# Routed expert works of two sizes, 256 and 128 rows, and three sets of split weights behind one staging tile

## The reference, cut to what matters

```python
scores = jnp.sqrt(jax.nn.softplus(flat @ gate_w))
_, indices = jax.lax.top_k(scores + gate_bias, 2)
weights = jnp.take_along_axis(scores, indices, axis=1)
weights = weights / jnp.clip(weights.sum(axis=-1, keepdims=True), 1e-06)
...
def _expert(xf, W1, W2, W3):                  # 192 -> 768 -> 192
    gate = jnp.minimum(xf @ W1, LIMIT)
    up = jnp.clip(xf @ W3, -LIMIT, LIMIT)
    return jax.nn.silu(gate) * up @ W2
y = _expert(flat, w1s, w2s, w3s)              # shared expert, all tokens
# plus, for each token, its two of eight experts, weighted
```

## Time and profile before

| | us |
|---|---|
| median of 3 runs | 557.76 |
| lowest, highest | 555.09, 557.76 |
| the profiled execution | 561.62 |
| its span | 559.8 |
| PE, DVE, ACT, POOL busy in it | 505.7, 375.3, 256.3, 229.4 |
| first routed matmul to the last result home | 130.6 to 317.95 |

### The profile page before, as it was taken

The page is one execution under the profiler, slowest core; times in us unless marked ns, Lnnn a source line. Parts: engine busy times, 40 slices in busy tenths (PEclk is TensorE's granted clock), DMA queues, the critical chain, the costliest instruction groups (busy, mean ns, idle before and its releaser), DMA issues.

```text
span 559.8 us, 9739 instructions
## 1 busy us (share of the span) xinstructions
PE 505.7 (90%) x3430; PEld 480.4 (86%) x3430; DVE 375.3 (67%) x892; ACT 256.3 (46%) x531; POOL 229.4 (41%) x194
## 2 busy tenths in 40 slices
PE   5799868779999999999999979999797788999996
PEld 5789768679999999999999869877576778999995
DVE  1576777356666666665666496799996766666665
ACT  0357471205554455544554214895761255353431
POOL 1404104715566657765666502488662100041300
PEclk9999998879999999999999989999998799999999
DMA  8750002753466567656673424000010200000001
GB/s 346 255 229 2 1 1 78 301 167 89 162 240 235 204 231 251 252 198 199 239 274 104 129 70 156 2 1 1 16 64 1 78 0 1 2 0 1 2 1 64
DMA packets 22634, 65.03 MB, mean 116 GB/s; under 512 B 6432, under 2 KB 15008, under 8 KB 19776
## 3 DMA queue, kind: packets, MB, share of 16 engines
q1 hardware_dynamic: 20192, 59.55, 30.4%
q0 software_dynamic: 2400, 4.93, 2.5%
HBM read 55.50 MB, written 8.97 MB: 115 GB/s over the span
## 4 chain that ended last, share of the span: by engine, by line
PE 72%; DVE 14%; issue 4%; ACT 4%; DMA 3%; POOL 2%; SPq 0%; DVEq 0%; POOLq 0%; ACTq 0%
PE psum L666 23%; PE psum L686 12%; PE psum L449 10%; PE psum L1077 4%; PE psum L466 3%; PE psum L833 3%; PE psum L1092 2%; PE psum L854 2%; PE psum L1109 2%; DVE AT L2029 2%; PE psum L1134 2%; DVE Y L1613 2%; PE psum L915 2%; PE psum L473 2%; DVE OW L2012 1%
## 5 line engine op out<-in xcount | busy, mean ns | idle before, releaser
L729 POOL TENSOR_TENSOR w0l<-stage,w0h 128x768 fp32r<-128x768 f32 x34 | 62.5, 1838 | 87.9 <-ACT w0h L713 82.0
L686 PE MATMUL psum<-w0d,a0h 128*128 128x192 f32 x492 | 86.8, 332 | 8.9 <-issue 6.6
L686 PEld LDWEIGHTS psum<-w0d,a0h 128*128 128x128 f32 x492 | 81.3, 194 | 11.4 <-issue 8.7
L761 DVE TENSOR_SCALAR a0t<-psum 128x256 f32<-128x256 f32 (+1 forms) x114 | 50.7, 445 | 47.8 <-PE psum L666 40.3
L740 ACT ACTIVATE psum<-psum 128x256 f32<-128x256 f32 x96 | 35.3, 368 | 85.0 <-PE psum L666 76.7
L666 PE MATMUL psum<-XWh,w0h 128*128 128x256 f32 x192 | 56.3, 293 | 0.0
L666 PE MATMUL psum<-XWh,w0t 128*128 128x256 f32 x192 | 54.4, 283 | 0.0
L666 PE MATMUL psum<-XWl,w0h 128*128 128x256 f32 x192 | 53.9, 281 | 0.0
L666 PE MATMUL psum<-XWl,w0t 128*128 128x256 f32 x192 | 53.8, 280 | 0.0
L666 PE MATMUL psum<-XWh,w0l 128*128 128x256 f32 x192 | 53.8, 280 | 0.0
L449 PE MATMUL psum<-X,w1h 128*128 128x384 f32 x144 | 49.6, 344 | 1.8 <-DVE a1hf L604 1.8
(11 more groups left out here) (261 smaller groups left out, 1264.6 us busy)
## 6 DMA issues: line engine op xcount, KB each, us to landing
stage<-moe0w SPq DMA_DIRECT2D x18, 1536.0 KB
w0d<-moe0d SPq DMA_DIRECT2D x18, 576.0 KB, 4.0
stage<-moe1w SPq DMA_DIRECT2D x4, 1056.0 KB, 5.0
marked_rows<-zero SPq DMA_DIRECT2D x4, 772.0 KB, 13.2
patch<-patches SPq DMA_DIRECT2D x4, 768.0 KB, 7.8
XR<-marked_rows SPq DMA_DIRECT2D x16, 192.0 KB, 3.6
G<-slots_out SPq DMA_DIRECT2D x6, 288.0 KB, 4.6
XR<-marked_rows SPq DMA_DIRECT2D x16, 65.0 KB, 3.8
```

Source lines behind the costliest of these rows:

```text
L686: last = nc.tensor.matmul(dst, A0["h"][qpar][:, fc, t * P:(t + 1) * P], W0[par]["down"][:, fc, :], start=(fc == these[0]), stop=(fc == the ...
L729: ins = engine.tensor_tensor(W0[par]["l"][:, mat, :], src, W0[par]["h"][:, mat, :].bitcast(F32), ALU.subtract)
L761: nc.vector.tensor_scalar(A0["t"][fc % 2][:, 0:width], bank[2 + fc % 2][:, 0:width], LIMIT, -LIMIT, ALU.min, ALU.max).then_inc(S0["clip_re ...
```

## The change

**Two sizes.** `WT` is 128 now, and the experts get whole blocks of 128 rows, `PARTS` = 25 of them. Eight works take two blocks each (wide, even numbers), nine take one (lone, odd numbers); they alternate, 17 in all. 3200 rows are computed where 4096 were. A longer table on VectorE (`wide_parts`, `lone_parts`, `experts`, `places`) finds the expert and the first block (`part`) of each work; SyncE reads both from it.

**A lone work** has its operands the other way round: the 128 rows are stationary and 384 columns of weights move (`e_rows_gate_up`), 20 matmuls. The product then lies with rows on partitions and is turned by six transposes (`e_turn`, in two halves) that ScalarE copies to `hT` (`e_turned`), before the down matmuls.

**Weights.** There are three sets of split weights (`w00`, `w01`, `w02`) and one staging tile of four pieces of 384 KB, each with a load and a semaphore of its own. Piece i of work n is loaded when the low part of piece i of work n - 1 is made. The low parts are counted by engine (`w_lo_pool`, `w_lo_dve`) and shared out by `low_engines`. Weights are loaded and split one work further ahead. The loops are written out, and the DMAs of the lone works' results are one each.

```diff
-WT = 256
-WORKS = (PICKS * TOK - E0) // WT + E0
-SLOTS = WORKS * WT
+WT = P
+PARTS = (PICKS * TOK - E0) // WT + E0
+WIDE = E0
+LONE = PARTS - 2 * WIDE
+WORKS = WIDE + LONE
+SLOTS = (PARTS + 2) * WT
...
+        def low_engines(n):
+            return {0: "pppp", 1: "vvvv", 2: "vvpp"}.get(n, "pppv" if n % 2 else "ppvv")
...
             def load_weights(n):
-                if n >= 2:
-                    sp.wait_ge(S["w_lo"], 4 * (n - 1))
...
+                for i in range(4):
+                    sp.wait_ge(*((S["w_lo_pool"], lows("p", n - 1, i)) if low_engines(n - 1)[i] == "p" else
+                                 (S["w_lo_dve"], lows("v", n - 1, i))))
+                    w = moe0w[0] if n == TAIL else moe0w[bass.ds(experts[n], 1)].rearrange("e p c -> (e p) c")
+                    sp.dma_start(stage[:, i, :], w[:, i * F0:(i + 1) * F0]).then_inc(ld_stage[i], 16)
...
             load_rows(1)
             load_rows(2)
-            for n in range(2, WORKS + 1):
-                if n > 2:
-                    load_rows(n)
-                load_weights(n + 1)
-                load_down(n)
-            load_down(TAIL)
+            load_weights(3)
+            load_rows(3)
+            for n in range(1, WORKS + 1):
+                if n + 3 <= TAIL:
+                    load_weights(n + 3)
+                if n + 3 <= WORKS:
+                    load_rows(n + 3)
+                load_down(n + 1)
...
+        def e_rows_gate_up(pe, u, n):
+            pe.wait_ge(x_lo, n)
+            for half in range(2):
...
+                for mat in range(2):
+                    wait_lows(pe, n, 2 * mat + 1)
+                    for i, (x, w) in enumerate(e_operands(1, None, W0[n % SETS],
+                                                          (slice(0, P), mat, slice(half * LH, (half + 1) * LH)))):
+                        last = nc.tensor.matmul(bank[2 * mat + half][:, 0:LH], x, w, start=(i == 0), stop=(i == 4))
+                last.then_inc(S0["gu_ready"], 1)
...
+            for n in range(1, WORKS + 1):              # ScalarE
+                u = units(n)
+                if n % 2:
+                    if n > 1:
+                        e_split_next(act, n + 2, 0)
+                        e_split_next(act, n + 2, 1)
+                    e_rows_silu(act, u, 0)
...
+            for n in range(3, TAIL + 1):               # GpSimd
                 if n > 4:
-                    pool.wait_ge(st_y[n % 2], 16 * (n - 4 + n % 2))
-                e_split_low(nc.gpsimd, pool, n, n % 2, range(3))
-                pool.wait_ge(S0["w_lo"], 4 * n + 3)
+                    pool.wait_ge(st_y[n % 2], sent(n - 4))
+                e_split_low(nc.gpsimd, pool, n)
+                pool.wait_ge(S0["w_lo_pool"], lows("p", n, 3))
                 if n > 3:
                     send_home(n - 3)
...
-            experts()
             e_product(dve, 0, 0, 5, CHW)
-            e_dve(dve, FC0, 1, CHW, None, None, None)
-            e_split_low(nc.vector, dve, 1, 1)
+            e_dve(dve, FC0, 1, CHW, None, {1: wide_parts, 2: lone_parts, 3: experts})
+            e_split_low(nc.vector, dve, 1)
+            places()
...
+            for n in range(1, WORKS + 1):              # VectorE
...
+                if n < WORKS:
+                    e_rows_low(dve, n + 1)
+                if n + 2 <= TAIL:
+                    e_split_low(nc.vector, dve, n + 2)
+                if n > 1:
+                    e_copy(dve, n - 1)
```

More of the change, by code:

```diff
@@ L53 @@
 XW1 = D + 1
-ZROWS = SLOTS // P // 4
+ZERO = 3
+ZROWS = SLOTS // P // ZERO
 SPARE = P * ZROWS
+RING3 = 3
 RING = (5, 6, 2)
@@ L208, in tower @@
         base = sb("base", [P, E0])
+        twos = sb("twos", [P, E0])
+        rest = sb("rest", [P, E0])
+        ends = sb("ends", [P, 2, 2, E0])
+        shift2 = sb("shift2", [P, 2, E0])
+        order = sb("order", [P, 2, LONE])
+        place = sb("place", [P, 2, LONE])
+        held = sb("held", [P, 2, LONE])
+        part = sb("part", [P, 2, LONE], I32)
         slot = sb("slot", [P, TILES * E0])
@@ L667, in e_gate_up, with e_turn, e_down @@
                 last.then_inc(S0["gu_ready"], 1)
[L669 to L673 removed]
+        def e_rows_gate_up(pe, u, n):
+            pe.wait_ge(x_lo, n)
+            for half in range(2):
+                if n == 1:
+                    pe.wait_ge(S0["silu_ready"], u + (half - 1))
+                else:
+                    pe.wait_ge(S0["h_ready"], u + (half - 2))
+                pe.wait_ge(S0["clip_ready"], u + (half - 1))
+                for mat in range(2):
[4 more added lines that the diff above has]
+                last.then_inc(S0["gu_ready"], 1)
+        def e_turn(pe, u, n, half):
+            pe.wait_ge(S0["h_ready"], u + (half + 1))
+            if half:
+                pe.wait_ge(h_out, turned_in(n) - 1)
+            for k in range(3):
+                last = nc.tensor.transpose(bank[7][:, k * P:(k + 1) * P], hR[:, half * LH + k * P:half * LH + (k + 1) * P],
+                                           ident)
+            last.then_inc(h_T, 1)
+        def e_down(pe, u, qpar, n, par, shared, ready, these=range(MOE0.fc)):
+            lone = not shared and n % 2
+            if lone:
+                pe.wait_ge(h_out, turned_in(n))
+            else:
+                pe.wait_ge(S0["h_ready"], u + these[-1] + 1)
+            pe.wait_ge(ld_w2[par], ready)
+            for t in range(3 if shared else 2 - par):
                 if shared:
@@ L715, in e_split_act, with e_split_next, e_split_low @@
                                  ACT.Copy).then_inc(S0["w_hi"], 1)
-        def e_split_low(engine, eng, n, par, parts=range(4)):
-            for i in parts:
+        def e_split_next(act, n, i):
+            if n <= TAIL:
+                e_split_act(act, n, i)
+        def e_split_low(engine, eng, n):
+            me = "p" if engine is nc.gpsimd else "v"
+            done = S0["w_lo_pool" if me == "p" else "w_lo_dve"]
+            w = W0[n % SETS]
+            for i in range(4):
+                if low_engines(n)[i] != me:
+                    continue
@@ L731, in e_split_low @@
-                ins.then_inc(S0["w_lo"], 1)
-        def e_act(act, u, width, following, rows, between={}, these=range(MOE0.fc)):
-            routed = width == WT
+                    dst = w["t"][64:P, mat, :]
+                    engine.tensor_tensor(dst, src[64:P], dst.bitcast(F32), ALU.subtract).then_inc(done, 1)
+                else:
+                    engine.tensor_tensor(w["l"][:, mat, :], src, w["h"][:, mat, :].bitcast(F32),
+                                         ALU.subtract).then_inc(done, 1)
@@ L736, in e_act @@
+        def e_act(act, u, width, between={}, these=range(MOE0.fc)):
+            routed = width == 2 * WT
             for fc in these:
                 act.wait_ge(S0["gu_ready"], u + (fc + 1))
-                if not routed and not (isinstance(u, int) and u == 0 and fc < 2):
+                if not routed and not (u == 0 and fc < 2):
                     act.wait_ge(S0["h_ready"], u + (fc - 1))
@@ L1014, in _ @@
+            e_gate_up(pe, TAIL_U, TAIL, 0, 2, range(AHEAD, AHEAD + 1))
+            e_down(pe, units(WORKS), 1, WORKS, 1, False, loaded(WORKS))
+            e_gate_up(pe, TAIL_U, TAIL, 0, 2, range(AHEAD + 1, FC0))
+            e_down(pe, TAIL_U, 0, TAIL, 0, True, loaded(TAIL), range(AHEAD, FC0))
             transposes(2, 0)
@@ L1318, in project @@
+            e_act(act, TAIL_U, CHW, these=range(AHEAD, FC0))
             def project(g):
@@ new lines, in _, with reached @@
+            lone_to, wide_to, lone_from, wide_from = (ends[:, i, k, :] for i in range(2) for k in range(2))
+            grid = [P, 2, LONE, E0]
+            def reached(to, side):
+                return nc.vector.tensor_tensor(
+                    to.rearrange("p (k w e) -> p k w e", k=2, e=E0),
+                    counts[:, 0:LONE].unsqueeze(1).unsqueeze(3).to_broadcast(grid),
+                    ends[:, side].unsqueeze(2).to_broadcast(grid), ALU.is_ge)
+            above, within = (rk[i][:, 0:2 * LONE * E0] for i in range(2))
```

456 lines of the change are left out of this document (267 added, 189 removed).

## The result

| | before | after |
|---|---|---|
| median, us | 557.6 | 579.28 |
| lowest, highest | 555.09, 557.76 | 574.82, 586.91 |
| ratio to before, with its 95% interval | | 1.0365, 1.0307 to 1.0424 |
| the profiled execution | 561.62 | 576.55 |
| first routed matmul | 130.6 | 127.4 |

The account below looks back on a forecast made before the run. TensorE bounds the kernel before; after the change a ring of 20.1 us a pair would. Works -4.9 and front -4 gave 552.7 for the profiled execution; 557.8 - 4.9 - 2 = 551 for the median, range 540 to 563.

Parts of the forecast that it names:

- TensorE does not stay the bound: In the routed works: TensorE's 17.8 us a pair lies below another limit of 20.1; TensorE staying the bound had chance 0.12.
- the ring: Routed works: a closed chain of waits through four engines, caused by the single staging tile, 20.1 us a pair.
- the landing of the result: Step in the ring: the indirect store of an odd work's result lands after 2.32 us, counted as 2.3.
- the slower rival: Routed works: result landing 2 us longer, pieces 1; 23.1 a pair, 24 us more; half likelier, 563; chance 0.2.
- VectorE's part: Steps in the ring: wide work's products and clips 2.2, low rows, low parts and copy 2.6, hand-overs 0.6.
- low parts and pieces: Steps in the ring: GpSimd's three low parts 5.8, VectorE's one 1.0, the load of the last two pieces 4.4.
- the charge of 1.0 for the shared port: Step in the ring: VectorE's one low part, free to meet GpSimd's under a port lock, charged in full at 1.0.
- too short for the clock: Routed works: TensorE waits some 2.4 us a pair in bits, too short to lower its clock.
- The front: Ahead of the routed works: an earlier start saves between 0 and 8 us, the middle of 4 taken.
- the hole: TensorE's slow stretch in the shared expert's down matmuls, until 116.23; gone in the forecast, kept in a rival, chance 0.2.
- The tail: The last, lone work, from its first matmul until its result is home: 19.4 us.
- its own sign of being wrong: In the changed profile: odd works' first matmuls over 21 us apart, with result landings of 3 or more.

Follow-up runs that it names:

- e1: Changed kernel with VectorE's copy of the last work's result ahead of its low parts of the weights; median 578.5 us, ratio 1.0325 to the kernel before.
- e10: e9 with the changed kernel's waits on GpSimd: each result sent by itself and each landing waited for; median 580.1 us, ratio 1.0394 to the kernel before.
- e9: e8 with the last two high parts of an odd work ahead of the copy of its second turned half; 555.6 us, ratio 0.9956 to the kernel before.
- e11: Changed kernel with only e9's ScalarE order, high parts behind activations; median 583.1 us, ratio 1.0435 to the kernel before.
- e12: The kernel before, run once more without an edit; 558.0 us, one execution.
- the first set: Four variants of the changed kernel, e1 to e4, run on one chip beside the kernel before; ratios 1.0325, 1.0832, 1.0127 and 1.0477 to it.
- e5: The changed kernel run again without an edit, on another chip; median 578.7 us, ratio 1.0396 to the kernel before.
- e8: e7 with ScalarE's high parts later: a place or two in even works, behind the activations in odd works; 561.3 us, ratio 1.0088 to the kernel before.
- e4: Changed kernel with two of an odd work's four low parts on GpSimd in place of three; median 589.2 us, ratio 1.0477 to the kernel before.
- e3: Changed kernel loading a quarter of each weight piece from work 4 on (stale weights); median 568.8 us, ratio 1.0127 to the kernel before.
- e7: e1's edit on the changed kernel, plus GpSimd waiting for result landings in one place a pair; 560.4 us, ratio 1.0091 to the kernel before.

## Why the prediction was wrong, point by point

**Right: TensorE does not stay the bound, and where the ring runs.** The order of places in the forecast (GpSimd low part, DMA of `stage`, ScalarE, VectorE, copy, home) is that of the measured round.

**Wrong in size: the landing of the result, 2.3 counted, 4.4 measured.** I took the store of the last work, which lands when no weights move. The earlier trace rows held the better row, 4.32, and the landings of that tile in the trace of before had a median of 4.6. I had put the 4.32 into the slower rival, at half its size. At its full size that rival's ring was 23.1 a pair, the measured one is 23.1, and its time would have been 575. That the two agree so well is luck: the rival had pieces landing 1 us later, which they did not, and left out the 2.5 us of the next point.

**Wrong in size: VectorE's part, 5.4 counted, 7.9 measured.** The two VectorE terms with the hand-overs were 2.2 + 2.6 + 0.6. In the round above, from VectorE's first product (284.95) to the store's issue (292.81) are 7.9. The chain names TensorE for 5.4 of it, but in VectorE's timeline no wait stands ahead of the copy:

```profile
288.52 2.05 DVE L850 TENSOR_TENSOR w<-stage,w 128x768 fp32r<-128x768 f32 x1
290.68 0.96 DVE L848 TENSOR_TENSOR w<-stage,w 64x768 fp32r<-64x768 f32 x1
291.66 0.36 DVE L941 COPY YO<-psum 128x192 f32<-128x192 f32 x1
```

The down matmuls of the odd work had ended at 289.45. The copy starts when the second low part is done, 0.02 to 0.04 us after it in all eight rounds. The two low parts took 3.1 (2.9 in the mean of the eight) where 1.9 was counted, since they meet GpSimd's. The products and clips took 3.2 where 2.2 was counted: they are seven and not five, and the last product waits for TensorE's last chunk (1.4) and its activation, a step that the forecast left out. The hand-over to GpSimd has the remaining 0.2. The net is +2.5. With the copy ahead of the low parts (e1) it waits for the down matmuls in their place, and the pair is 1.8 shorter.

**Nearly right: low parts and pieces.** 6.8 was counted for the low parts and 6.4 measured, 4.4 for the piece and 3.5 measured. Of the charge of 1.0 for the shared port, 0.5 stands in the ring on GpSimd (2.36 for 1.84). Together: 20.1 + 2.1 + 2.5 - 0.4 - 0.9 = 23.4, the round above is 23.3.

**Missed: a second bound.** In the kernel's text GpSimd waits until its own indirect stores have landed before it goes on, so each landing is a part of its list: five low parts, three issues and two waits for landings, 21 to 22 us a pair. e10 beside e9 shows it, 21.9 against 19.7. In the changed kernel it was hidden behind the ring. With all as changed a pair is 23.1, with the copy first 21.3, with one landing less 20.9, with the order of ScalarE 20.5 and 19.7. With the order of ScalarE alone (e11) it is 23.1 again, and with only the two landings left (e10) 21.9. Whether GpSimd's wait could be left out altogether, no run tried.

**Wrong: "too short for the clock".** The longest of TensorE's stops in the works is 4.0 us, the next 3.2, since ScalarE waits for a piece ahead of the activations of an odd work; then come one of 2.6 and fifteen of 1 to 1.8. Windows of 2 us of the changed kernel, then TensorE's down matmuls in its timeline (start, us):

```profile
270.00:272.00 2.00, 0.00 (x0) 0.00 (x0) 0.00 (x0) 0.83 (x2) 0.49 (x1) 1.00 0.99 383
...
274.00:276.00 2.00, 2.00 (x8) 2.00 (x7) 1.28 (x3) 1.14 (x3) 1.86 (x2) 0.50 0.18 71
276.00:278.00 2.00, 2.00 (x10) 2.00 (x9) 0.88 (x2) 0.00 (x0) 2.00 (x1) 0.67 0.43 100
```

```profile
273.42 5.75 PE L798 MATMUL psum<-w0d,a0h 128*128 128x192 f32 x24
```

TensorE stopped from 269 to 273, the clock is 0.50 from 274 to 276 and 0.67 from 276 to 278, and 24 down matmuls that take 3.90 in the earlier trace rows take 5.75. The clock was as low in three more stretches, from 164 to 172, 188 to 192 and 226 to 230; ahead of the first of them stand stops of 1.5 and 1.6 us. I had none of it.

**The front: -4 forecast, -3.2 in the first traces, nothing that lasts.** In its first trace the changed kernel has no stop of TensorE in the scatter. It stops behind it, for the rows (TensorE's timeline, the idle time and what ended it in the bracket):

```profile
122.78 0.69 PE L816 MATMUL psum<-const,XR 128*128 128x128 f32 x2 [4.77 <-DMA XR<-marked_rows]
123.92 3.79 PE L798 MATMUL psum<-w0d,a0h 128*128 128x192 f32 x12 [0.45 <-DVE a0h L898]
```

The forecast for a start without the hole was 122.5. The rows came 3.3 later than the 119.5 counted, and the 12 down matmuls cost 3.5 where 1.95 was counted, at a clock of 0.54 from 120 to 124 and 0.61 from 124 to 128. The chain of waits runs through VectorE's list there, `places` (112.3 to 115.1) included, so that table was not wholly hidden under the scatter. And the kernel before can start at 126.1 (e12), while the changed one started at 127.4 and 129.3. Variants of it started at 138 in the first set, with matmuls that come one by one (the timeline of TensorE in e1, idle time in the bracket):

```profile
108.60 0.32 PE L798 MATMUL psum<-w0d,a0h 128*128 128x192 f32 x1 [0.62 <-issue]
110.00 0.32 PE L798 MATMUL psum<-w0d,a0h 128*128 128x192 f32 x1 [1.07 <-issue]
```

A matmul of 0.32 us each 1.4 us, with an idle time that no semaphore ends: this is the hole of the earlier trace rows, some 10 us long. It came with the chip or the execution, as far as the runs tell, and in the kernel before too. The trace doesn't name what TensorE waits for. I had named heavy DMA traffic as what it follows, and e5 to e8 have the same traffic without a hole, while e1 to e4 and e9 to e11 have it. Loads of instructions don't explain it: e1's trace has none between 96.4 and 120.8, and the matmuls come without a gap again from 119.2. The cause is open.

**The tail and the rest.** From the last odd work's first matmul at 312.4 to 333.5 are 21.1 us, where 19.4 were forecast. The eight pairs were 185.0 where 163 were forecast. With the front at -3.2 that is 561.6 + 18.7 - 3.2 = 577.1, and the profiled execution took 576.55.

**The ranges.** The chance for the slower side was 0.2, with its price cut in half by a choice that no row supported. The range ended there. The forecast had named its own sign of being wrong, a distance over 21 with result landings of 3 or more, and that is what came.

## What to carry to other kernels

Take the size of a wait from its median in the busy stretch, never from the last one of a program, and write the ring down with every engine that a result passes, the one with slack too. When a change makes the bounding engine faster, list for each other engine what it does in one period including what it waits out in its own queue: here a second bound of 21 to 22 us lay behind the ring. The copy's place alone gave 1.8 us a pair, the order on ScalarE alone nothing. The saved matmuls (22.9 to 17.8 a pair by count) came out only as far as the lists of the other engines were put in a fitting order, all three edits together (23.1 to 19.7).

## What the runs showed of the hardware

An indirect store of 96 KB from GpSimd lands in 2.3 us when no weights move, in 2.8 (median) with traffic of 136 GB/s (e3) and in 4.3 to 4.6 in most runs among loads of weights at 193 to 249 GB/s (3.7 in e8 and 5.1 in e10). The Trainium skill (DMA: Bandwidth & Descriptors, Anatomy of one DMA) gives 2.0 us plus bytes over 436e3, by which an estimate is 2.2: the store without traffic agrees, the one among loads takes twice that. Where a GpSimd and a VectorE low part of 64 rows meet, the one takes up to 2.4 in place of 1.84 and the other up to 2.5 in place of 0.96. After a stop of 4 us the granted clock was 0.50 for two us and 0.67 for two more, and 24 matmuls cost 1.9 more. The start of the works differed by 10 us between executions on different chips with the same text ahead of them (e4 and e7), through a stretch in which TensorE issued one matmul per 1.4 us.
